# A residual block with linear attention in fp32 pieces: the split of wo, its check and the first product with it move to later chunks

## What is computed

```python
def attn(y):                        # y = layernorm(x), no gain
    n = layernorm(y) * ln1_g + ln1_b
    q, k, v = n @ wq, n @ wk, n @ wv          # 256 x 256 each, 16 heads of 16
    phi_q, phi_k = elu(q) + 1, elu(k) + 1
    kv = einsum('bshd,bshe->bhde', phi_k, v)  # sums over all 4096 rows
    z = phi_k.sum(over s)
    y = y + (phi_q @ kv / (phi_q . z + 1e-6)) @ wo
    h = layernorm(y) * ln2_g + ln2_b
    return y + table_gelu(round((h @ w1) / 0.1)) @ w2    # 256 -> 1024 -> 256
x = x + attn(layernorm(x))
x = x + (layernorm(x) @ CB.T) * (SCB / 127) + bias
```

## Time and profile before

| | us |
|---|---|
| median of 3 runs | 569.27 |
| lowest, highest | 568.08, 572.17 |
| the profiled execution | 567.73 |
| its span, first to last instruction | 565.9 |
| PE busy in it | 533.6 (94%) |
| DVE, ACT, POOL busy | 451.6, 396.5, 344.9 (80%, 70%, 61%) |

### The profile page before, as it was taken

One profiled execution on the slowest core, in us unless ns is written; L12 is line 12 of the kernel. 1 busy time (PEld: TensorE's weight loads), 2 busy tenths in 40 slices (PEclk: granted clock), 3 DMA queues, 4 the chain that ended last, 5 costly groups with the idle time before them and its releaser, 6 DMA issues.

```text
span 565.9 us, 11319 instructions
## 1 busy us (share of the span) xinstructions
PE 533.6 (94%) x3610; PEld 485.9 (86%) x3610; DVE 451.6 (80%) x1059; ACT 396.5 (70%) x656; POOL 344.9 (61%) x336
## 2 busy tenths in 40 slices
PE   6899999899989899999999999999999999999885
PEld 6789998798878788989898898988989889898775
DVE  5899998899777588886978879788787878879636
ACT  2587874656558587876968768687776878768760
POOL 3344336142222578687686877768787786877654
PEclk9899998999999999999999999999999999999999
DMA  7423111211101011010201202012020210200001
GB/s 267 143 75 111 58 54 39 69 43 38 38 23 38 1 39 43 32 75 0 74 37 37 74 2 74 37 37 74 0 74 0 74 49 25 74 0 39 37 1 77
DMA packets 11419, 29.47 MB, mean 52 GB/s; under 512 B 2048, under 2 KB 4864, under 8 KB 11392
## 3 DMA queue, kind: packets, MB, share of 16 engines
q1 hardware_dynamic: 9472, 28.32, 14.1%
q10 hardware_dynamic: 1920, 0.79, 0.6%
HBM read 20.71 MB, written 8.39 MB: 51 GB/s over the span
## 4 chain that ended last, share of the span: by engine, by line
PE 68%; DVE 15%; issue 8%; POOL 4%; ACT 2%; DMA 2%; DVEq 0%; POOLq 0%; SPq 0%; ACTq 0%
PE psum L1021 61%; PE psum L1039 5%; DVE bn_stats_b L684 3%; DMA f_arena<-in_L_attn_x_dram 2%; DVE f32r_arena L837 2%; PE psum L1060 2%; POOL f32r_arena L383 2%; DVE f32r_arena L829 2%; DVE mean_var L691 1%; DVE bn_stats L684 1%; DVE n_and_ones L711 1%; ACT f_arena L612 1%; DVE f_arena L711 1%; ACT f32r_arena L614 1%; DVE f_arena L874 1%
## 5 line engine op out<-in xcount | busy, mean ns | idle before, releaser
L1021 PE MATMUL psum<-w_hi,f32r_arena 128*128 128x256 f32 x1280 | 174.3, 282 | 4.7 <-POOL f32r_arena L383 3.0
L1021 PEld LDWEIGHTS psum<-w_hi,f32r_arena 128*128 128x128 f32 x1280 | 164.1, 188 | 14.0 <-issue 5.8
L1021 PE MATMUL psum<-f32r_arena,w_hi 128*128 128x512 f32 x512 | 141.1, 402 | 1.4 <-issue 1.4
L383 POOL TENSOR_TENSOR f32r_arena<-f_arena,f32r_arena 128x512 fp32r<-128x512 f32 x64 | 85.5, 1336 | 82.6 <-ACT f32r_arena L614 46.4
L601 ACT ACTIVATE grid_index<-psum,w_bias_in_steps 128x512 int8<-128x512 f32 x128 | 87.2, 681 | 50.8 <-PE psum L1021 50.7
L1021 PEld LDWEIGHTS psum<-f32r_arena,w_hi 128*128 128x128 f32 x512 | 88.1, 188 | 14.8 <-issue 1.6
L612 ACT ACTIVATE f_arena<-grid_index 128x512 f32<-128x512 int8 x128 | 80.9, 632 | 24.7 <-POOL f32r_arena L383 16.4
L614 ACT ACTIVATE f32r_arena<-grid_index 128x512 fp32r<-128x512 int8 x128 | 79.2, 619 | 0.0
L1021 PE MATMUL psum<-f32r_arena 128*128 128x256 f32 (+1 forms) x384 | 70.7, 334 | 2.5 <-DVE f32r_arena L723 1.9
L1021 PEld LDWEIGHTS psum<-f32r_arena 128*128 128x128 f32 x384 | 56.8, 195 | 7.9 <-issue 3.0
L829 DVE TENSOR_TENSOR f32r_arena<-f_arena,f32r_arena 128x512 fp32r<-128x512 f32 x64 | 57.9, 905 | 1.2 <-ACT f32r_arena L614 1.2
(11 more groups left out here) (117 smaller groups left out, 872.0 us busy)
## 6 DMA issues: line engine op xcount, KB each, us to landing
f_arena<-in_L_attn_x_dram SPq DMA_DIRECT2D x32, 512.0 KB, 3.3
out_dram<-f_arena SPq DMA_DIRECT2D x15, 512.0 KB, 2.7
f_arena<-in_L_attn_w_dram SPq DMA_DIRECT2D x2, 1024.0 KB, 12.6
out_dram<-f_arena SPq DMA_DIRECT2D x2, 256.0 KB, 2.1
phi_q<-in_L_attn_wk_dram ACTq DMA_DIRECT2D x1, 256.0 KB, 4.7
phi_q<-in_L_attn_wq_dram SPq DMA_DIRECT2D x1, 256.0 KB, 4.9
phi_q<-in_L_ffn_CB_dram SPq DMA_DIRECT2D x1, 256.0 KB, 7.2
phi_q<-in_L_attn_wo_dram SPq DMA_DIRECT2D x1, 256.0 KB, 8.0
```

The costliest lines, as they stand in the source:

```text
L383: nc.gpsimd.tensor_tensor(t_lo[m % SLOTS], tf[m % 2], t_hi[m % SLOTS].bitcast(F32), ALU.subtract).then_inc(s["t_lo_p"], 1)
L1021: return nc.tensor.matmul(out_, lhs, rhs, start=start, stop=stop, skip_group_check=True)
```

## The change

Three moves, all in the unrolled half of phase 1. On GpSimd the split of wo additionally waits until the rows of chunk 10 are normalised. On DVE its check moves from the end of chunk 8 to chunk 9, between `low1(10)` and `phi_query(9)`; the reading of the flag's value moves from chunk 9 to chunk 10, behind `finalize(0)`. On PE the flag's transpose moves from chunk 9 to chunk 10, between `gather(10, 0)` and the attention product, and its wait is for chunk 10's `phi_key` there, since bank 4 must be read; the wait for `flag2` moves with it to chunk 11's keys. Chunk 0's product with wo goes from before `gather(13, 1)` to behind it. No operation is added or removed but the one wait.

```diff
@@ GpSimd, pair @@
                     if is_chunk(c, PER_SEQ):
+                        g.wait_ge(s["n1_ready"], c + 3)
                         split_wo()
@@ DVE @@
+            def wo_column():
+                v.wait_ge(s["wo_lo_done"], KT)
+                ve.tensor_reduce(flag_cols[:, 2 + SLICES:3 + SLICES], wo_lo[:, :].bitcast(F32), AX.X, ALU.max,
+                                 apply_absolute_value=True).then_inc(s["wo_flag"], 1)
+                v.wait_ge(s["wo_flag"], 1)
+                v.wait_ge(s["w_flag"], SLICES)
+                flag_column(2, SLICES + 1, 4 + SLICES)
@@ DVE, pair @@
                     phi_key(c, 0)
                     phi_key(c, 1)
-                    if is_chunk(c, PER_SEQ + 1):
-                        flag_value(PP, 2, "flag2")
                     if within(c + 1):
                         high1(c + 1, 1 - p)
                         low1(c + 1, 1 - p)
+                    if is_chunk(c, PER_SEQ + 1):
+                        wo_column()
                     if is_chunk(c, PER_SEQ + 2):
                         finalize(0, TP + 1)
+                        flag_value(PP, 2, "flag2")
...
                     if within(c + 2):
                         norm1(c + 2, p)
-                    if is_chunk(c, PER_SEQ):
-                    if is_chunk(c, PER_SEQ):
-                        v.wait_ge(s["wo_lo_done"], KT)
-                        ve.tensor_reduce(flag_cols[:, 2 + SLICES:3 + SLICES], wo_lo[:, :].bitcast(F32), AX.X, ALU.max,
-                                         apply_absolute_value=True).then_inc(s["wo_flag"], 1)
-                        v.wait_ge(s["wo_flag"], 1)
-                        v.wait_ge(s["w_flag"], SLICES)
-                        flag_column(2, SLICES + 1, 4 + SLICES)
@@ PE, key_pair @@
-                    if is_chunk(n, 2 * (PER_SEQ + 2)):
+                    if is_chunk(n, 2 * (PER_SEQ + 3)):
                         pe.wait_ge(s["flag2"], 1)
@@ PE, pair @@
                         if is_chunk(c, PER_SEQ + 1):
                             pe.wait_ge(s["a1_ready"], c + 2)
                             turn_sums(0, TP)
+                        if is_chunk(c, PER_SEQ + 2):
                             pe.wait_ge(s["flag_max"], 2)
                             pe.wait_ge(s["phi_k_done"], 2 * c + 3)
                             turn_flag(4 + SLICES, PP)
-                        if is_chunk(c, PER_SEQ + 2):
                             pe.wait_ge(s["a1_ready"], c + 2)
                             pe.wait_ge(s["kv_ready"], 1)
                             attention(0, 0, 0)
...
+                        gather(c, p, 1)
                         if is_chunk(c, PER_SEQ + 5):
                             pe.wait_ge(s["a1_ready"], c + 2)
                             pe.wait_ge(s["wo_lo_done"], KT)
                             attention_out(0, True)
-                        gather(c, p, 1)
```

## The result

| | before | changed |
|---|---|---|
| median, first set (4 runs each) | 569.45 us | 563.87 us |
| lowest, highest | 568.08, 572.17 | 562.76, 564.85 |
| ratio, 95% interval | | 0.9896 (0.9853 to 0.9938) |
| ratio in two later sets (11 and 9 runs of the change) | | 0.9931 (0.9911 to 0.9950), 0.9927 (0.9899 to 0.9955) |
| the profiled execution, its span | 567.73, 565.9 | 564.48, 562.8 |

The change is faster by about 0.7% (1.0% in the first set). The profiled executions differ by 3.25 us. Over all executions, the medians are 568.58 us (89 of the kernel before, its copy among them) and 564.54 us (26 of the changed one): 4.0 us. The two later sets ran on two different chips, and each ratio compares only within its set: there the medians differ by 5.6, 3.9 and 4.8 us.

The account below looks back on a forecast made before the run. PE was taken to bound the kernel (68% of the chain), with little idle near the edits. Terms -1.64 + 0.3 - 0.80 = -2.1 us took the median from 569.27 to 567.2 us; range 564.6 to 569.9 us.

Parts of the forecast that it names:

- the end of the split: GpSimd's split of wo, started at 98.1 us, would end at about 104.6 us, or 102.8 us if not shut out.
- the first half: Split and check of wo moved: chunk 11's transposes start at 108.95 us instead of 110.59 us, 1.64 us gained.
- part 4: Product with wo behind gather(13,1): PE's wait for the residual L851 before chunk 15's transposes goes, 0.80 us gained.
- Part 1 and 2: Later split, check in chunk 9: PE waits of 0.7, 0.25 and 0.54 us in chunks 9 and 10 go.
- remaining idle: Before chunk 11's transposes PE would still idle about 1.1 us, as DVE normalises that chunk late.
- part 1: Split waits for chunk 10's rows: without the GpSimd collision DVE normalises them sooner, removing PE's 0.7 us wait.
- Part 3: Flag's transpose and value moved to chunk 10: DVE's normalising comes late and PE waits, 0.3 us lost (bounds 0 and 0.7).
- Phase 2 moves as a whole: Phase 2 waits for nothing anchored to a clock time, its loads being issued behind the gathers, so it only shifts.
- a changed clock: A lower granted clock behind changed gaps, named as an unseen possible cause of a change above 1%.

Follow-up runs that it names:

- its copy: The kernel before run again unchanged against itself: 568.57 us (12 runs), ratio 1.0001 (0.9986 to 1.0017).
- the wait only: The kernel before with only GpSimd's added wait ahead of the split of wo, its check left at the end of chunk 8: 573.88 us, ratio 1.0088.

## Why the prediction was wrong

The mechanisms of the sum were right but for the worth of the added wait; its sizes were not. The step that failed most is the end of the split in the -1.64 us of the first half (104.6 us taken, 103.85 measured), which came out as 2.46 us; then the -0.80 us of part 4, which is 1.14 us. With them the sum is 3.5 us at equal clocks, where I had 2.1. That alone would have put the median at 565.8 us, inside the range. That the first set's median lies below the range takes a second step, the way from one trace to the median, and what makes up that rest stays open.

**The terms of the sum, with equal clocks** (the two profiled executions, from start to start on PE):

| step | forecast | measured |
|---|---|---|
| before chunk 11's transposes | -1.64 | -2.46 (25.65 to 23.19) |
| flag in chunk 10 | +0.3 | +0.11 (10.01 to 10.12) |
| before chunk 15's transposes | -0.80 | -0.96 (11.94 to 10.98) |
| from there to the next transposes | 0 | -0.18 (8.29 to 8.11) |
| sum | -2.1 | -3.5 |

- *Part 1 and 2, PE's own readiness.* PE's idle was taken from the bracket in front of the matmuls (0.7 + 0.25 + 0.54 us), with 0.11 us for the flag's transpose. That bracket begins at a modelled end, before which the next matmul can start: in the changed kernel chunk 10's transposes start at 98.62 us, the key products ahead of them end at 96.52 + 2.26 = 98.78. From start to start the same three steps are 0.89 us (2.99 to 2.10 from the key products to chunk 10's transposes), 0.47 us on to the gather and 1.11 us on to the next key products: 2.47 us, where I had 1.60. The weight loads' brackets, of which I read 0.94, 0.68 and 0.92 us in the trace and did not use, were nearer.
- *The end of the split, the step that set the 1.64 us.* It ends at 104.05 us, less the 0.2 us of offset 103.85, where I took 104.6. I let GpSimd be shut out of both L355 for as long as the cast and L723 run. The rows show one L355 at 1.44 us and the other at 0.79, and DVE's two delayed by 0.4 us together: both sides give. (The sum on from there, 104.6 + 0.8 + 1.93, is 107.3 us and not the 107.5 that I wrote; measured, those steps took 2.8 us.) With PE ready 0.9 us sooner than counted and the rows of chunk 11 0.8 us sooner, the 1.0 us of remaining idle came out as forecast, by two errors of one size.
- *That the added wait is what pays* was my part 1, 0.7 us, and as a mechanism wrong. Without it the trace gives 23.30 us instead of 23.19. The collision is hidden by the idle before chunk 11, which I named myself as the next bound, without drawing the conclusion.
- *Part 3* lost 0.11 us and not 0.3: L735 of chunk 10 started late and L711 still came in time. *Part 4* was the right mechanism, 0.96 us and not 0.80, for the same reason as above, and 0.18 us behind it that I did not look for.
- *Phase 2 moves as a whole*: its first product starts 3.5 us sooner (168.31 and 164.79 us), and from there to the end of the span it is 397.6 us before, 398.0 us changed. Other traces of either kernel have 397.4 to 398.3 us where the last store is not late, so these 0.4 us are spread.

**From the trace to the median.** I carried the 2.1 us over unchanged, as if one execution stood for all. The trace stood for those in which the clock is low for 3.4 us in chunk 8. There the change gives 25.65 - 23.19 = 2.5 us before chunk 11; in executions without the fall it gives 27.25 - 21.51 = 5.7 us. The prediction named a changed clock only as a cause that it could not see, for the chances beyond 1%. That the split in the kernel before also holds PE when the clock is high was a question that the earlier trace rows could have raised: no row of the split there waits for PE. Yet this does not account for the medians, since the changed kernel also has executions with 6.8 us of low clock. By the means of the traces (five of six of the kernel before with the 3.4 us; of the changed one two with 3.4, two with 6.8, one without) the stretch gains 25.91 - 23.53 = 2.4 us, with part 4 and the flag 3.4 us, against 4.0 us between the medians. The intervals of both later sets take in 3.4 us (2.8 to 5.1 and 2.6 to 5.8 us), so that the runs differ by more than the traces is not shown. The remaining 0.6 us, the 1.6 us by which the first set's medians differ more than that 4.0, the share of each kind among the timed runs, and why 6.8 us was seen in the changed kernel and its kin but in none of six traces of the one before, stay open.

## What to carry to other kernels

Read PE's idle from start to start against an undisturbed round of the same work, not from the bracket behind modelled ends. Ask of each wait what it becomes if the engine waited for is early or PE is faster: a helper that ends at its own time turns every gain into idle. And before a moved instruction is credited with a collision that it avoids, look whether the idle behind it would have paid for it.

## What the hardware showed beyond that

- Between equal executions of one kernel the granted clock in chunk 8 was at half for 0, 3.4 or 6.8 us, worth 11.80, 13.48 or 15.15 us between two sets of transposes.
- An idle of 2.6 to 4.7 us on PE in chunk 9 was followed by low clock in the gather behind it in all four traces that had one (gather of 3.02 to 3.59 us, otherwise 1.90 to 2.00). One of the four, the wait only, had the low stretch of chunk 8 as well.
- DVE and GpSimd do not simply shut one another out: in the changed kernel a cast took 0.95 instead of 0.69 us and a subtract 1.38 instead of 1.22, while two L355 took 0.79 and 1.44 instead of 0.5 to 0.6 us. By the Trainium skill (SBUF — State Buffer, "SBUF: two separate sides") one fully blocks for whole instructions; each of these delays fits a wait for the other's current instruction, but neither engine kept the other out over two instructions in a row, as in the 2.07 us of the earlier trace rows.
- The last store adds to the spread: from DVE's last instruction to the end of the span 2.5 us (changed, 564.24 us), 2.6 us (before, 567.73 us), 4.1 us (before, 571.98 us) and 4.8 us (changed, 565.38 us). This is why the changed execution with full clock is not the shortest of the traced ones.
